# Loads of an attention kernel split in two and issued, with the stores, at four points of a turn; setup constants issued by ScalarE

## What is computed

```python
B, F, E = x.shape                      # 2048, 40, 64
q = (einsum('bfe,oe->bfo', x, Wq) + bq).reshape(B, F, H, D)   # H = 4, D = 32
k = (einsum('bfe,oe->bfo', x, Wk) + bk).reshape(B, F, H, D)
v = (einsum('bfe,oe->bfo', x, Wv) + bv).reshape(B, F, H, D)
att = einsum('bfhd,bghd->bhfg', q, k) / sqrt(E)
att = softmax(att, axis=-1)
out = einsum('bhfg,bghd->bfhd', att, v).reshape(B, F, H * D)
return relu(out + einsum('bfe,oe->bfo', x, Wr) + br)
```

## Time and profile before

| | us |
|---|---|
| median of 3 runs | 953.42 (952.27 to 956.1) |
| profiled execution, device time | 954.55 |
| its span, first to last instruction | 952.8 |
| PE busy | 916.7 (96%) |
| POOL busy | 877.5 (92%) |
| ACT busy | 770.5 (81%) |
| DVE busy | 727.1 (76%) |
| DMA data queue, share of 16 engines | 34.5% |
| granted TensorE clock, mean | 0.996 |

### The profile page before, as it was taken

How to read it: one execution, slowest core, us unless ns; L and a number is a source line. 1 busy time by engine, 2 the same in 40 slices (tenths; PEclk the granted TensorE clock), 3 DMA queues, 4 the chain that set the end, 5 groups by cost and what they waited for, 6 DMA issues and landing times.

```text
span 952.8 us, 68655 instructions
## 1 busy us (share of the span) xinstructions
PE 916.7 (96%) x30720; PEld 681.0 (71%) x30720; DVE 727.1 (76%) x2066; ACT 770.5 (81%) x1541; POOL 877.5 (92%) x1028
## 2 busy tenths in 40 slices
PE   4999999999999999999999999999999999999996
PEld 3777777777677777777777777777777777777774
DVE  4777777777787777777777777777777778777785
ACT  3888888888787887888888888888888888888886
POOL 2999999999898998999999999999999999999997
PEclk9999999999999999999999999999999999999998
DMA  3333333333333333333433333333333333334321
GB/s 105 92 116 102 113 108 108 115 102 113 100 115 100 111 103 101 114 112 104 115 102 113 106 109 116 101 114 102 113 107 108 108 107 116 103 112 113 103 80 65
DMA packets 63336, 101.18 MB, mean 106 GB/s; under 512 B 9536, under 2 KB 42560, under 8 KB 63040
## 3 DMA queue, kind: packets, MB, share of 16 engines
q1 hardware_dynamic: 63040, 96.79, 34.5%
HBM read 54.81 MB, written 41.94 MB: 102 GB/s over the span
## 4 chain that ended last, share of the span: by engine, by line
PE 96%; issue 2%; DMA 1%; DVE 0%; POOL 0%; SPq 0%; ACT 0%; POOLq 0%; ACTq 0%
PE vr_bank L408 23%; PE o_bank L440 22%; PE s_buf L385 19%; PE o_bank L365 14%; PE s_buf L417 10%; PE vr_bank L398 6%; PE vr_bank L410 1%; DMA vr_bias<-vr_bias_in 1%; PE o_bank L369 0%; POOL y_sum L174 0%; POOL m_diag L166 0%; ACT y_rows L217 0%; POOLq L35 0%; PE vr_bank L403 0%; DVE s_buf L304 0%
## 5 line engine op out<-in xcount | busy, mean ns | idle before, releaser
L166 POOL TENSOR_TENSOR m_diag<-m_split,ident 128x640 bf16<-128x640 bf16 x256 | 322.3, 1259 | 54.8 <-DVE m_split L315 40.6
L174 POOL TENSOR_TENSOR y_sum<-rv,y_att 128x512 f32<-128x512 f32 x256 | 303.8, 1187 | 1.5 <-DVE y_att L326 1.5
L182 POOL TENSOR_SCALAR q_bd<-q_flat,consts 128x320 f32<-128x320 f32 x512 | 266.5, 534 | 15.4 <-ACT q_flat L210 13.2
L408 PE MATMUL vr_bank<-w_cols,xT 64*128 64x128 f32 x2048 | 270.6, 273 | 0.0
L410 PE MATMUL vr_bank<-w_cols,xT 64*128 64x128 f32 x2048 | 270.6, 273 | 0.0
L237 ACT ACTIVATE rv<-vr_bank 128x1024 f32<-128x1024 f32 x256 | 260.6, 1018 | 0.0
L304 DVE TRANSPOSE_TENSOR_REDUCE s_buf<-s_buf 128x20 f32<-128x640 f32 x256 | 221.5, 865 | 46.6 <-PE s_buf L385 46.6
L408 PEld LDWEIGHTS vr_bank<-w_cols,xT 64*128 64x128 f32 x2048 | 251.2, 190 | 0.4 <-issue 0.4
L410 PEld LDWEIGHTS vr_bank<-w_cols,xT 64*128 64x128 f32 x2048 | 250.3, 189 | 0.0
L440 PE MATMUL o_bank<-rv,pT 64*40 64x33 f32 x16384 | 225.9, 202 | 14.6 <-issue 13.1
L385 PEld LDWEIGHTS s_buf<-q_bd,kT 64*40 64x40 f32 x8192 | 150.8, 113 | 116.6 <-issue 116.3
(11 more groups left out here) (33 smaller groups left out, 623.8 us busy)
## 6 DMA issues: line engine op xcount, KB each, us to landing
xT<-xT_in SPq DMA_DIRECT2D x256, 208.0 KB, 2.5
y<-y_rows SPq DMA_DIRECT2D x512, 80.0 KB
w_cols<-w_in SPq DMA_DIRECT2D x1, 128.0 KB, 2.0
vr_bias<-vr_bias_in SPq DMA_DIRECT2D x1, 128.0 KB, 5.1
consts<-consts_in SPq DMA_DIRECT2D x1, 20.0 KB, 2.7
biases<-bias_in SPq DMA_DIRECT2D x1, 1.0 KB, 1.8
```

What stands on the lines that cost most here:

```text
L166: pool.tensor_tensor(m_diag[:], m_split[:, place % 2].unsqueeze(2).to_broadcast([P, BLOCKS, QUAD]), ident[:].unsqueeze(1).to_broadcast([P, ...
L174: pool.tensor_tensor(y_sum[:, n % 3].rearrange("r (a d) -> r a d", d=DIM), rv[:, place % 4, 1, :, 0:DIM], y_att[:, place % 2].rearrange("r ...
L182: pool.tensor_scalar(q_bd[:, place % 4, :, s], q_flat[:, place % 2].rearrange("d (b f) -> d b f", f=FIELDS), consts[:, C_HEAD + s:C_HEAD + ...
L408: nc.tensor.matmul(vr_bank[:, 0, OUT * pair:OUT * (pair + 1)], xT[0:HALF, place % 8, cols], w_cols[0:HALF, 1], start=False, stop=True, ski ...
```

## The change

Loads are cut in two halves of 64 partitions. In SP's turn the four DMAs now stand apart: first half of the load when `vr_made` rises, first store when `y_ready` has risen, second half of the load when `o_made` says that attend of the running PE turn has ended, second store when `shifted` says the same of the shift. In setup, `consts`, `vr_bias` and `biases` are issued by ACT ahead of everything else it does; `w_cols` counts on a semaphore of its own; the first projections of PE wait for that and for x of turn 0 alone, and PE's wait for `prepared` and the new `set_up` stands ahead of the first L398 (L419 after). DVE makes `ident` and `pick` behind the bias terms.

```diff
         @block.sync
         def _(sp):
-            sp.dma_start(w_cols[:], w_in).then_inc(loaded, 16)
-            sp.dma_start(biases[:], bias_in).then_inc(loaded, 16)
-            sp.dma_start(consts[:], const_in).then_inc(loaded, 16)
-            def load(n, place):
-                sp.dma_start(xT[:, place % 8, 0:PAD], xT_in[n]).then_inc(x_loaded[place % 8], 16)
-            load(0, 0)
-            load(1, 1)
-            sp.dma_start(vr_bias[:], vr_bias_in.to_broadcast([P, 2, OUT])).then_inc(loaded, 16)
+            sp.dma_start(w_cols[:], w_in).then_inc(weights, 16)
+            def load(n, place, lane):
+                sp.dma_start(xT[lane:lane + HALF, place % 8, 0:PAD], xT_in[n, lane:lane + HALF]).then_inc(x_loaded[place % 8], 16)
...
             def group(n, place):
                 if exists(n + 8):
                     sp.wait_ge(vr_made, n + 1)
-                    load(n + 8, place)
+                    load(n + 8, place, 0)
                 if not before(n, 5):
-                    store(n - 5, place + 3)
+                    store(n - 5, place + 3, 0)
+                if exists(n + 8):
+                    if not before(n, 2):
+                        sp.wait_ge(o_made, n - 1)
+                    load(n + 8, place, HALF)
+                if not before(n, 5):
+                    sp.wait_ge(shifted, n)
+                    store(n - 5, place + 3, 1)
...
         @block.scalar
         def _(act):
+            act.dma_start(consts[:], const_in).then_inc(loaded, 16)
+            act.dma_start(vr_bias[:], vr_bias_in.to_broadcast([P, 2, OUT])).then_inc(loaded, 16)
+            act.dma_start(biases[:], bias_in).then_inc(loaded, 16)
             act.wait_ge(loaded, LOADS)
...
                 if not before(n, 1):
                     pe.wait_ge(vr_ready, n)
+                else:
+                    pe.wait_ge(prepared, PREPARED)
+                    pe.wait_ge(set_up, SET_UP)
...
-            pe.wait_ge(loaded, LOADS)
-            pe.wait_ge(prepared, PREPARED)
+            pe.wait_ge(weights, 16)
```

More of the change, by code:

```diff
@@ L81, in attention_kernel @@
         o_part = o_bank[:, :, 0:8 * VW].rearrange("r c (a v) -> r c a v", v=VW)
+        weights = sem("weights")
         loaded = sem("loaded")
         prepared = sem("prepared")
+        set_up = sem("set_up")
         x_loaded = [sem(f"x_loaded{i}") for i in range(8)]
@@ L105, in attention_kernel @@
         y_stored = [sem(f"y_stored{i}") for i in range(4)]
-        LOADS = 16 * 4
+        LOADS = 16 * 3
         LAG = 3
-        PREPARED = 13
+        PREPARED = 10
+        SET_UP = 3
         def run(group):
@@ L128, in _, with store @@
         def _(sp):
-            sp.dma_start(w_cols[:], w_in).then_inc(loaded, 16)
-            sp.dma_start(biases[:], bias_in).then_inc(loaded, 16)
-            sp.dma_start(consts[:], const_in).then_inc(loaded, 16)
-            def load(n, place):
-                sp.dma_start(xT[:, place % 8, 0:PAD], xT_in[n]).then_inc(x_loaded[place % 8], 16)
-            load(0, 0)
-            load(1, 1)
-            sp.dma_start(vr_bias[:], vr_bias_in.to_broadcast([P, 2, OUT])).then_inc(loaded, 16)
-            for n in range(2, 8):
[L140 to L145, removed]
+            sp.dma_start(w_cols[:], w_in).then_inc(weights, 16)
+            def load(n, place, lane):
+                sp.dma_start(xT[lane:lane + HALF, place % 8, 0:PAD], xT_in[n, lane:lane + HALF]).then_inc(x_loaded[place % 8], 16)
+            for n in range(2):
+                load(n, n, 0)
+                load(n, n, HALF)
+            for n in range(2, 8):
+                load(n, n, 0)
+                load(n, n, HALF)
+            def store(n, place, g):
+                if g == 0:
+                    sp.wait_ge(y_ready, n + 1)
+                sp.dma_start(out[n, g], y_rows[HALF * g:HALF * g + FIELDS, place % 4]).then_inc(y_stored[place % 4], 16)
             def group(n, place):
@@ L149, in group @@
                     sp.wait_ge(vr_made, n + 1)
-                    load(n + 8, place)
+                    load(n + 8, place, 0)
                 if not before(n, 5):
-                    store(n - 5, place + 3)
+                    store(n - 5, place + 3, 0)
[6 more added lines that the diff above has]
+                    store(n - 5, place + 3, 1)
             run(group)
             for n in range(STEPS - 5, STEPS):
-                store(n, n)
+                store(n, n, 0)
+                store(n, n, 1)
             for place in range(4):
@@ L192, in _ @@
             pool.wait_ge(prepared, PREPARED)
+            pool.wait_ge(set_up, SET_UP)
             run(group)
@@ L264, in _ @@
         def _(dve):
+            nc.vector.memset(m_swap[:].rearrange("r i b -> r (i b)"), 0.0).then_inc(prepared, 1)
             for buf in s_buf:
@@ L270, in _ @@
             dve.wait_ge(loaded, LOADS)
[L271 to L277, removed]
             nc.vector.tensor_tensor(out_bias[:], vr_bias[:, 0], vr_bias[:, 1], ALU.add).then_inc(bias_made, 1)
@@ L295, in _ @@
             nc.vector.tensor_copy(bias_rows[:], bias_row[:].unsqueeze(1).to_broadcast([P, 2, OUT])).then_inc(prepared, 1)
+            nc.vector.tensor_copy(ident[:], consts[:, C_PICK:C_PICK + QUAD]).then_inc(set_up, 1)
+            dve.wait_ge(bias_made, 1)
+            for member in range(MEMBERS):
+                nc.vector.tensor_copy(pick[:, member, 0:FIELDS],
+                                      consts[:, C_MEMBER + member:C_MEMBER + member + 1].to_broadcast([P, FIELDS]))\
+                    .then_inc(set_up, 1)
             def keys(n, place):
@@ L358, in queries_and_keys @@
                 if n == 0:
-                    pe.wait_ge(x_loaded[0], 16)
+                    pe.wait_ge(x_loaded[0], 32)
                 elif before(n, LAG + 1):
@@ L400, in values_and_residual @@
                 if exists(n + 1):
-                    pe.wait_ge(x_loaded[(place + 1) % 8], 16 * turn_of(n + 1, place + 1, 8))
+                    pe.wait_ge(x_loaded[(place + 1) % 8], 32 * turn_of(n + 1, place + 1, 8))
                 nc.tensor.matmul(vr_bank[:, 1].rearrange("r (m j c) -> r m j c", m=MEMBERS, j=2)[:, :, 1],
```

## The result

The changed kernel takes 941.0 us (median of 4 runs, 936.22 to 944.5) against 952.85 us (4 runs, 951.71 to 956.1): a ratio of 0.9892, 95% interval 0.9849 to 0.9934. It is faster by 1.1%, as forecast in sign, with half of the size: 12 us where 21 were forecast.

A forecast was written before the change was run, and what follows sets the result against it. PE bounds the kernel, with 31.2 us lost in stops for instruction blocks. 954.55 us of the profiled execution - 18.7 (spreading) - 3.0 (setup) = 932.8, with the median 1.1 lower: 932 us, range 919 to 954.

The forecast's parts named there:

- What bounds the kernel: PE, busy 96% of the span; 31.2 us lost in long turns as PE waits for its next instruction block.
- Size: Steady turns: spreading the data wins back 0.6 of the 31.2 us lost in stops, -18.7 us.
- the sum 1.13 + 1.47 + 1.40: Fetch loop at an attend stop: resumption to fetch, transfer, fetch end to resumption; 4.00 us against 3.60 between blocks.
- the 1.47 us transfer overlapped no data: Instruction fetch at an attend stop: it ran after the data had ended, so its length is not plain queueing.
- Packets follow an issue by about 0.9 us: DMA bursts of a turn: with this delay the first half load and store run at offsets 1.1 to 2.1 us.
- Twice the load DMAs: cost 0: SP's turn: 256 more issues of 0.36 us each, some 1.5 us of issue a turn, hidden by SP's idle time.
- Setup: Start of the kernel: constants land near 6.2 us and first projections run during the bias chain; -3.0 us, bounds 0 to -6.
- The +0.2 us for slow matmuls: Setup on PE: matmuls may stay slow a little longer after an early start and a pause; +0 to +0.6, taken +0.2.
- The first (stops stay, 950 us): Steady turns: fetch length and latency are not due to data, so spacing does nothing; 950.4 us, chance 0.2.
- The second (slower): Steady turns: the second burst hits the fetch and lengthens the loop at attend boundaries; 970 us, chance 0.1.
- The third (half loads cost as much as whole ones, 940 us): Loads: 64 partitions take as long as 128, so only a third of the stops go; 940 us, chance 0.1.

The follow-up runs named there:

- pad_to_128: The changed kernel with eight one-column matmuls more in each turn, making 128 matmuls a turn; 985.17 us in one execution.
- no_data: The changed kernel without loads of turns 8 to 255 and without stores of turns 0 to 251; 927.3 us, ratio 0.9773.
- spread_only: The kernel before with the steady loads split and loads and stores spread as in the change, setup as before; 941.36 us, ratio 0.9916.
- bunched: The changed kernel with all four DMAs of a turn issued right behind the end of PE's turn, split but not spread; 952.43 us, ratio 1.0029.
- setup_only: The changed kernel with the turns' loads and stores put back as before, only the new setup left; 947.26 us, ratio 0.9975.
- queue_only: The kernel before with only consts, vr_bias and biases issued by ACT; 947.15 us in one execution.
- first_only: The changed kernel without the second pair of DMAs of each turn, from turn 8 up to the last four stores; 934.57 us, ratio 0.985.
- load_then_stores: The changed kernel with one whole load at the end of PE's turn and both stores when the shift has ended; 943.01 us, ratio 0.9899.
- early: The changed kernel with the second pair of DMAs released by the end of the scores instead of attend and shift; 951.44 us, ratio 1.0015.
- stores_then_load_2: Repeat of the changed kernel with both stores at the end of PE's turn and the whole load after attend; 941.34 us, ratio 0.9914.

## Why the prediction was right and wrong

**What bounds the kernel: right.** PE ended the chain, the loss lay in stops at the ends of 128-matmul blocks, shown by pad_to_128, and data placing moves it, shown by no_data, spread_only and bunched against the rest.

**The step that failed is "Size": 0.6 of the 31.2 us.** In place of -18.7 us the profiled execution gave -6.3, spread_only -8.8 in medians. The direction was right; the fraction was a choice between two ends, 0 and 31.2 us, and the measured gain is nearer to 0. Three things were off. First, 31.2 us was one execution: setup_only and queue_only, with the same whole loads and bunched stores, lost 26.9. Second, 7 us cannot be had by any placing, as no_data shows, so the end at -31.2 us was out of reach. Third, the data in the spread order still costs about 13 us (940.3 against 927.3 us); the pair ahead of the fetch has the larger part of it, as first_only shows, although the prediction had taken it to be out of the way. Under this lies the sum 1.13 + 1.47 + 1.40: it let every tenth saved in a term shorten the loop, while loops of 4.00 us were measured with fetches that ended 0.3 us apart. The prediction's own warning, that the 1.47 us transfer overlapped no data, should have weighed more: in no_data too transfers reach 1.54 us.

**"Packets follow an issue by about 0.9 us" did not carry over.** The half load's issue takes 0.48 us in the median instead of 0.36, and 0.97 us in the turn shown, and packets began 1.9 us into that turn, 1.4 us in turns without a stop, for 1.1 forecast. "Twice the load DMAs: cost 0" put SP's issues at 1.5 us a turn; they take 1.98 us. Where all four DMAs go at once this costs: bunched is about 5 us over setup_only. In the spread order no cost of it is shown, since load_then_stores, with one whole load, has the changed kernel's ratio.

**Setup: right, 1.5 us too small by the profiles.** Turn 2 came 4.55 us earlier, for -3.0 forecast, though setup_only shows 2.9 us in medians: the constants landed at 5.34 us instead of 6.2, and the bias chain covered the first projections as forecast. The +0.2 us for slow matmuls can't be seen: the bias matmul took 0.37 us after and 0.42 before.

**The rivals.** The first (stops stay, 950 us) is refuted as it stood by spread_only and no_data, but it had a part of the truth: a quarter of the loss, 7.1 of 27 to 31 us, is there without data, and so are long transfers. The second (slower) did not happen to this kernel. In early, whose second burst does run beside the fetch, the loss came back, but no more than that: 951.44 us, not 970. The third (half loads cost as much as whole ones, 940 us) has the time that was measured, by luck: load_then_stores and stores_then_load_2, with whole loads, are no faster than the changed kernel, so half loads are not what kept the gain small. The Trainium skill's rule in "DMA: Bandwidth & Descriptors" ("Rules for kernel authors") against two transfers to disjoint partition halves agrees with bunched, which is slower than whole loads. Nothing here speaks against it: the gain comes from the spreading, and whole loads have it as well.

## What to carry to other kernels

Where PE works through many small matmuls without a pause, look for a queue named "instruction" and for idle time on "issue" whose place moves by a fixed number of instructions a turn; then DMA traffic that never delays a tensor can still cost time. Spread the data so that it stays clear of the fetch after the densest stretch (one wait in the middle of the turn did that here, without splitting a load), but first run the kernel without its data: that tells how much any placing can give. And when a loop is so near a tie, one profile of the loss is not a size; take several, and forecast a fraction only from a run with the suspected cause removed.

## What the runs showed of the hardware

- A 16 KB fetch of PE's instructions took 0.88 to 1.44 us of transfer at attend's boundaries in no_data, with almost no other DMA. Where PE stopped for a block, it had spent 3.7 to 3.75 or 4.0 to 4.05 us since the block before (128 matmuls) in most cases, with data and without; it went on 1.43 to 1.44 us after the fetch had ended, in the median, in the changed kernel, in no_data and in the kernel before.
- Without loads and stores 7.1 us were lost in such stops, without loads 7.7, with all data bunched 26.9 to 32.5.
- The issue of a 64-row load took 0.48 us on SP (median), that of a 128-row load 0.36 us, that of the 88- and 40-row loads 0.29 us.
- The same program lost 15.6, 20.5 and 25.0 us in long turns in three profiled executions at nearly the same granted clock (0.997, 0.997 and 0.995).
